# Sums of squares by head in the second layer of a four-layer transformer kernel: the head columns as stationary operand

## The reference, cut to what matters

```python
# B, L = 8, 256; H = 16 heads of 32; xin is the modulated layer norm of x
qkv = (xin @ Wqkv.T + qkv_bias).reshape(Bs, Lx, 3, H, D)
...
sm = jnp.exp(jnp.minimum(scale_mul_log, jnp.log(jnp.float32(100.0))))
qn = q / jnp.maximum(jnp.linalg.norm(q, axis=-1, keepdims=True), 1e-12) * sm
kn = k / jnp.maximum(jnp.linalg.norm(k, axis=-1, keepdims=True), 1e-12)
scores = jnp.einsum('bhqd,bhkd->bhqk', qn, kn) + attn_bias
p = jax.nn.softmax(scores, axis=-1)
```

## Time and profile before

| | |
|---|---|
| median of 3 runs | 2158.23 us (2153.22 to 2158.89) |
| the profiled execution | 2151.35 us, of which 2149.6 us are the span of the trace |
| PE busy | 1930.4 us, 90% |
| DVE, ACT, POOL busy | 1132.2, 1029.0, 785.8 us (53%, 48%, 37%) |
| mean granted clock of TensorE | 0.953 |
| the 32 chains of layer 1 | from 658 to 1589 us of the span |

### The profile page before, as it was taken

The page is one execution under the profiler, slowest core; times in us unless marked ns, Lnnn a source line. Parts: engine busy times, 40 slices in busy tenths (PEclk is TensorE's granted clock), DMA queues, the critical chain, the costliest instruction groups (busy, mean ns, idle before and its releaser), DMA issues.

```text
span 2149.6 us, 34826 instructions
## 1 busy us (share of the span) xinstructions
PE 1930.4 (90%) x12744; PEld 1512.8 (70%) x12744; DVE 1132.2 (53%) x3157; ACT 1029.0 (48%) x2450; POOL 785.8 (37%) x1093
## 2 busy tenths in 40 slices
PE   4778999999999999999899999979999989977875
PEld 2556777777888878788678777768875768745453
DVE  4656432653553365435674675574554675456442
ACT  3533332343333344443465465555567456477753
POOL 4454553211112443233577453336331432233220
PEclk9889999999999999999899999999999989989988
DMA  7234666545445533345345433424433424322310
GB/s 264 64 128 147 216 206 225 191 157 188 163 173 180 184 133 127 133 157 196 133 167 174 156 123 133 149 91 151 141 118 128 163 80 171 120 77 79 98 60 30
DMA packets 95097, 310.35 MB, mean 144 GB/s; under 512 B 10576, under 2 KB 11344, under 8 KB 93392
## 3 DMA queue, kind: packets, MB, share of 16 engines
q1 hardware_dynamic: 94928, 308.12, 41.4%
HBM read 241.50 MB, written 66.58 MB: 143 GB/s over the span
## 4 chain that ended last, share of the span: by engine, by line
PE 65%; DVE 13%; issue 7%; ACT 6%; POOL 6%; DMA 2%; SPq 0%; POOLq 0%; DVEq 0%; ACTq 0%
PE B L183 59%; PE B L186 6%; DVE SS L207 2%; DVE FB L204 2%; DMA ST<-in_wpack 2%; ACT SS L189 2%; POOL SS L198 1%; ACT FB L189 1%; POOL W L201 1%; POOL R L201 1%; DVE T L201 1%; DVE PT L195 1%; DVE FB L201 1%; ACT L189 1%; POOL W L198 1%
## 5 line engine op out<-in xcount | busy, mean ns | idle before, releaser
L198 POOL TENSOR_SCALAR SS<-SS,NM 128x256 f32<-128x256 f32 (+1 forms) x640 | 290.0, 470 | 829.4 <-DVE NM L213 829.3
L183 PE MATMUL B<-HM,W 128*128 128x512 f32 x2304 | 538.6, 394 | 15.6 <-DVE HM L204 8.7
L183 PEld LDWEIGHTS B<-HM,W 128*128 128x128 f32 x2304 | 438.8, 191 | 110.3 <-DVE HM L204 9.5
L183 PE MATMUL B<-G,W 128*128 128x512 f32 x1536 | 404.0, 414 | 29.7 <-DVE FB L204 9.8
L183 PEld LDWEIGHTS B<-G,W 128*128 128x128 f32 x1536 | 292.9, 196 | 103.9 <-issue 20.8
L189 ACT ACTIVATE SS<-SS,NM 128x256 f32<-128x256 f32 (+1 forms) x512 | 240.6, 471 | 218.1 <-DVE NM L198 217.8
L183 PE MATMUL B<-HA,W 128*128 128x512 f32 x864 | 222.3, 408 | 7.9 <-DVE HA L201 5.9
L186 PE MATMUL B<-ident,SS 128*128 128x128 f32 x1152 | 179.2, 294 | 40.3 <-POOL SS L198 27.8
L183 PEld LDWEIGHTS B<-HA,W 128*128 128x128 f32 x864 | 165.6, 196 | 46.9 <-DVE HA L201 6.3
L186 PEld LDWEIGHTS B<-ident,SS 128*128 128x128 f32 x1152 | 129.8, 147 | 76.1 <-POOL SS L198 34.2
L201 DVE TENSOR_TENSOR G<-FB,G 128x512 fp32r<-128x512 f32 x128 | 101.3, 793 | 155.2 <-ACT G L189 155.1
(11 more groups left out here) (108 smaller groups left out, 2658.7 us busy)
## 6 DMA issues: line engine op xcount, KB each, us to landing
W<-kept SPq DMA_DIRECT2D x357, 512.0 KB, 4.3
kept<-W SPq DMA_DIRECT2D x119, 512.0 KB, 4.6
ST<-in_wpack SPq DMA_DIRECT2D x135, 256.0 KB, 3.0
Y<-in_adaw SPq DMA_DIRECT2D x12, 1024.0 KB, 6.4
out_xT<-X SPq DMA_DIRECT2D x16, 256.0 KB, 2.1
X<-in_xT SPq DMA_DIRECT2D x1, 3072.0 KB, 14.6
FB<-in_pos SPq DMA_DIRECT2D x4, 256.0 KB, 7.6
X<-in_xT SPq DMA_DIRECT2D x1, 1024.0 KB, 6.7
```

Of the source, the lines that this page charges most:

```text
L183: return self.real.matmul(*a, **k) if self.real is not None else self
L198: return self.real.tensor_scalar(*a, **k) if self.real is not None else self
```

## The change

The sum of squares of a head is made with the operands exchanged. The head columns, padded by zeros to 32, are the stationary operand; each of the four 128x128 blocks of squares is the moving one, and the four results go to the four groups of 32 partitions of one bank, one column tile each. The sums then have the heads on the partitions, so two things are added: VectorE copies the 128x128 result into the scratch tile g, and PE transposes it once. The maximum that writes R16 reads 4 of each 32 columns of the transposed bank. The work is now in two steps, `sums` and `un2`. The head columns get a tile of their own (a view of CT, which is free by then) and a transfer of 16 KB in the step "bias". The positions of the q, k and v steps of layer 1 in `PLACE` are new.

```diff
-    "q1": [-1.273, 0.351, 1.427],
-    "k1": [0.902, 1.089, 2.211, 2.301, 3.616],
-    "v1": [3.958, 4.1],
+    "q1": [-1.372, -0.577, 0.6, 1.483],
+    "k1": [1.287, 0.51, 0.837, 2.25, 2.391, 3.618],
+    "v1": [3.809, 4.1],
...
             self.banked("un1", k, f, g)
             yield
+            self.banked("sums", k, g)
+            yield
             self.banked("un2", k, g)
...
+        heads = CT[:, 0, 0, :]
...
+                elif kind == "sums":
+                    k, g, u = a
+                    bank, sq = dp.buf(u), fr.buf(g)
+                    e.wait_ge(*s_heads.of())
+                    e.wait_ge(*a_qsq.of(*k))
+                    e.wait_ge(*dp.over(u))
+                    for j in range(4):
+                        r = e.matmul(bank[32 * j:32 * j + 32, 0:128], heads, sq[:, 128 * j:128 * j + 128],
+                                     start=True, stop=True)
+                    r.then_inc(*p_ss.up(*k))
                 elif kind == "un2":
                     k, g, u = a
-                    bank, sq = dp.buf(u), fr.buf(g)
-                    e.wait_ge(*a_qsq.of(*k))
+                    e.wait_ge(*d_ss.of(*k))
                     e.wait_ge(*dp.over(u))
-                    for m in range(4):
-                        r = e.matmul(bank[:, 4 * m:4 * m + 4], sq[:, 128 * m:128 * m + 128],
-                                     CV[:, COLS["head"]:COLS["head"] + 4], start=True, stop=True)
-                    r.then_inc(*p_ss.up(*k))
+                    e.transpose(dp.buf(u)[:, 0:128], fr.buf(g)[:, 0:128], ident[:, :]).then_inc(*p_sst.up(*k))
...
+                elif kind == "sums":
+                    k, g, u = a
+                    e.wait_ge(*p_ss.of(*k))
+                    e.tensor_copy(fr.buf(g)[:, 0:128], dp.buf(u)[:, 0:128]).then_inc(*d_ss.up(*k))
+                    dp.done(u, d_ss, *k)
...
-                    e.tensor_scalar(R16[:, x, 0, :], dp.buf(u)[:, 0:16], 1e-24, None, ALU.max).then_inc(*d_qmax.up(*k))
+                    e.tensor_scalar(R16[:, x, 0, :].rearrange("p (j h) -> p j h", j=4),
+                                    dp.buf(u)[:, 0:128].rearrange("p (j h) -> p j h", j=4)[:, :, 0:4], 1e-24, None,
+                                    ALU.max).then_inc(*d_qmax.up(*k))
...
+                    e.dma_start(heads, headsd).then_inc(*s_heads.up())
```

More of the change, by code:

```diff
@@ L70, in _cols @@
                     ("bfc1", 16), ("bfc2", 4), ("bada2", 8), ("emb_b", 8), ("ln_g", 4), ("ln_b", 4), ("out_b", 4),
-                    ("b1", 16), ("b2", 4), ("sml", 4), ("invf", 1), ("head", 4), ("quarter", 1)):
+                    ("b1", 16), ("b2", 4), ("sml", 4), ("invf", 1), ("quarter", 1)):
         COLS[name] = at
@@ L657, in spread, with program @@
         return out
-def program(nc, xT, pos, condT, biasd, cols, consts, tab2, wpack, adaw, out):
+def program(nc, xT, pos, condT, biasd, cols, consts, headsd, tab2, wpack, adaw, out):
     ctx = ExitStack()
@@ L721, in program @@
         s_st = [tally(f"s_st{k}", 16) for k in range(STAGES)]
-        s_ad, s_cv, s_ct, s_id, s_rot = (tally(x, 16) for x in ("s_ad", "s_cv", "s_ct", "s_id", "s_rot"))
+        s_ad, s_cv, s_ct, s_id, s_heads, s_rot = (tally(x, 16) for x in ("s_ad", "s_cv", "s_ct", "s_id", "s_heads", "s_rot"))
         p_adt, d_ad = tally("p_adt"), tally("d_ad")
@@ L726, in program @@
         p_ada, p_tot, p_var, p_bc = (tally(x) for x in ("p_ada", "p_tot", "p_var", "p_bc"))
-        p_qkv, p_rot, p_ss, p_nb = (tally(x) for x in ("p_qkv", "p_rot", "p_ss", "p_nb"))
+        p_qkv, p_rot, p_ss, p_sst, p_nb = (tally(x) for x in ("p_qkv", "p_rot", "p_ss", "p_sst", "p_nb"))
         p_sc, p_tr, p_va, p_out = (tally(x) for x in ("p_sc", "p_tr", "p_va", "p_out"))
@@ L742, in program @@
         d_trig, d_sin, d_qk, d_qhi, d_khi = (tally(x) for x in ("d_trig", "d_sin", "d_qk", "d_qhi", "d_khi"))
-        d_klo, d_qmax, d_ck = tally("d_klo"), tally("d_qmax"), tally("d_ck")
+        d_klo, d_ss, d_qmax, d_ck = tally("d_klo"), tally("d_ss"), tally("d_qmax"), tally("d_ck")
         d_max, d_neg, d_rec, d_pt, d_cx = (tally(x) for x in ("d_max", "d_neg", "d_rec", "d_pt", "d_cx"))
@@ L751, in program @@
         tallies = [
-            s_const, s_x0, s_x, s_pos, s_tab, s_out, *s_st, s_ad, s_cv, s_ct, s_id, s_rot, p_adt, d_ad, *s_w, p_ada, p_tot, p_var, p_bc, p_qkv, p_rot, p_ss,
+            s_const, s_x0, s_x, s_pos, s_tab, s_out, *s_st, s_ad, s_cv, s_ct, s_id, s_heads, s_rot, p_adt, d_ad, *s_w, p_ada, p_tot, p_var, p_bc, p_qkv, p_rot, p_ss, p_sst,
             p_nb, p_sc, p_tr, p_va, p_out, p_up, p_down, p_first, p_second, p_last, a_silu, a_sm, a_sq,
@@ L755, in program @@
             a_y, d_ada, d_sm, d_gb, d_sum, d_sub, d_sq, d_var, d_nmul, d_nlo, d_trig,
-            d_sin, d_qk, d_qhi, d_khi, d_klo, d_qmax, d_ck, d_max, d_neg, d_rec, d_pt, d_cx, d_xo, d_gate, d_glo,
+            d_sin, d_qk, d_qhi, d_khi, d_klo, d_ss, d_qmax, d_ck, d_max, d_neg, d_rec, d_pt, d_cx, d_xo, d_gate, d_glo,
             d_xd, d_tg, d_xl, g_const, g_whi, g_wlo, g_rstd, g_cos, g_qlo, g_qr, g_norm, g_xb]
@@ L1250, in vector @@
                     x = 0 if k[0] == "q" else 1
-                    e.wait_ge(*p_ss.of(*k))
+                    e.wait_ge(*p_sst.of(*k))
                     if k[2:] != (0, 0):
                         e.wait_ge(*a_wide.of(k[0], 1, *divmod(4 * k[2] + k[3] - 1, 4)))
-                    e.tensor_scalar(R16[:, x, 0, :], dp.buf(u)[:, 0:16], 1e-24, None, ALU.max).then_inc(*d_qmax.up(*k))
+                    e.tensor_scalar(R16[:, x, 0, :].rearrange("p (j h) -> p j h", j=4),
+                                    dp.buf(u)[:, 0:128].rearrange("p (j h) -> p j h", j=4)[:, :, 0:4], 1e-24, None,
+                                    ALU.max).then_inc(*d_qmax.up(*k))
                     dp.done(u, d_qmax, *k)
@@ L1812 @@
         _vec(g["L3_cond_b1"].reshape(-1)), _vec(g["L3_cond_b2"].reshape(-1)), _vec(rep),
-        np.tile(inv, 4)[:, None], np.repeat(np.eye(4, dtype=f), 32, axis=0),
+        np.tile(inv, 4)[:, None],
         np.full((128, 1), math.pi / 2)], axis=1)
@@ L1838 @@
         "cols": np.ascontiguousarray(cols.astype(f)),
-        "consts": consts, "tab2": tab2, "wpack": wpack, "adaw": adaw,
+        "consts": consts, "headsd": np.repeat(np.eye(4, 32, dtype=f), 32, axis=0), "tab2": tab2, "wpack": wpack, "adaw": adaw,
     }
```

## The result

| | before | after |
|---|---|---|
| median | 2153.59 us (6 runs, 2147.18 to 2158.89) | 2167.38 us (6 runs, 2165.94 to 2168.82) |
| profiled execution | 2151.35 us | 2167.59 us |
| mean granted clock | 0.953 | 0.947 |

The ratio is 1.0067, with a 95% interval of 1.0054 to 1.0079: slower by 0.67%, some 14 us. The forecast was 2160 us and "no change". The time lies in the range that holds 8 in 10 (2147 to 2171) and 2.4 us above the forecast's own range (2152 to 2165). The call was wrong: the difference is a little over twice what can be told from nothing.

What follows compares the result with a forecast made beforehand. PE, busy 90% of the span, was taken as the bound; 10.9 us spared against 13.8 us of waits, at 77%, gave +2.2 us, on a 2158.2 us median 2160 us, "no change"; own range 2152 to 2165, 8 in 10 2147 to 2171.

Steps and rivals of the forecast that it cites:

- the sum: Balance of PE time spared (10.9 us) against added waits (13.8 us), each passed on at 77%: +2.2 us.
- The sums on TensorE: PE's block of 8 passes in four column tiles takes 0.35 us, not 0.81; 0.17 us of it fixed.
- The transpose: PE's added transpose in each of 32 chains: 0.12 us, 0.20 as upper end where it stands alone between products.
- The waits: PE waits 5.5 us before `un3` at four queries and 4.3 us before `sums` at keys right behind their product.
- the lag: DVE starts R<-B or the key's copy late, adding 0 to 1.9 us wherever little lies between; taken as 4 us.
- the four short queries: Places 1 and 2, piece 2 tile 3, piece 1 tile 3: PE waits 1.75, 1.85, 1.15, 0.8 us before `un3`.
- rival 2: Slower: DVE's lag at its upper end, about 11 us, waits passed on in full; +10 us, 2168 us; chance 0.20.
- The pass-on at 77%: Only 77% of spared time and waits reaches the end, PE's share of the first stretch's last-ending chain.
- Rival 1: Faster: the waits don't stand where put, at most a third come; 2143 to 2151 us, middle 2149; chance 0.29.
- rival 3: Slower or no gain: column tiles of a block of 8 don't overlap; +11, about 2170 us; chance 0.06.

Runs made afterwards that it cites:

- e2: The changed kernel at the positions of before, with the exchanged operands alone, no copy and no transpose (numbers wrong): ratio 0.9960 to the kernel before.
- e11: The changed kernel with the query's `un2` and `un3` back at their positions of before: 2173.9 us, ratio 1.0099 to the kernel before.
- e12: e11 with ACT issuing the query's spread behind the key's two activations instead of before them: 2156 us, ratio 1.0012 to the kernel before.
- e3: The whole change at the positions of before, with the `sums` steps added: 2177.4 us, ratio 1.0115 to the kernel before.
- e1: The kernel before, with the old sums, at the new query, key and value positions: 2174.7 us, ratio 1.0100 to the kernel before.
- e5: The kernel before with the query's new positions alone: ratio 1.0058 to the kernel before.
- e6: The kernel before with the key's new positions alone: ratio 1.0013 to the kernel before.
- e8: The change for the queries only, at the positions of before, keys keeping the old sums: 2147.5 us, ratio 0.9979 to the kernel before.

## Why the prediction was right and wrong

**The measured size lies in the range, the call "no change" was wrong**, and the failed step is the sum: its waits were too small, and a cost of the clock was not in it. It was 10.9 us spared against 13.8 us of waits, both passed on at 77%: -8.4 + 10.6 = +2.2 us. In the stage it is 5.6 us less work and 16.8 us more idle time, +11.2.

That the time lies in the range is in part luck. 2160 us stands on the median of three runs, 2158.2. The median of six is 2153.6; from there the forecast is 2156 and its wide range ends at 2166, below the measured 2167.4. The change forecast was +2 us, the measured one is +13.8.

*The sums on TensorE: right.* 0.35 us a block were taken; it is 0.36 before a product and 0.24 before B<-PT,V. The four column tiles overlap. The drain of the Trainium skill's page "TensorEngine Tiling (Array Packing)", "Key Properties", never costs more here than the 0.17 us a block that the rows before had shown: the whole block takes 0.24 to 0.36 us. At nine of the 32 places B<-PT,V follows, which has the same tiling.

*The transpose: within its bounds on the whole.* 0.12 us were taken, 0.20 as the upper end. A lone one takes 0.02 to 0.03 us from start to start between products and 0.27 before a wait, and at the full clock the kernels with transposes have 0.3 to 2.4 us more work than e2 for all 32 of them. The sign that was named, PE's busy time falling by 10 us or more, did not come: it fell by 5.6 us in the stage and rose from 1930.4 to 1931.5 over the span. Outside the stage it is 6.7 us more, and there lie 17 of the 28 us more at the lower clock.

*The waits: right in kind, short in size, and one link was missing.* Foretold were 5.5 us before `un3` and 4.3 us before the sums; measured are 9.6 us more before B<-ident,FB, 7.3 before B<-FB,CT, and 4.2 before B<-few,T in the stage, which had no price: 21.1 against 13.8 with the lag. At the four short queries PE waits 0.91, 2.81, 2.26 and 1.42 us, 7.4 in all, but three of the four are released by DVE's CX and only one (2.26, at place 2) by the spread. I counted PE's work between `un2` and `un3` against the chain through DVE, POOL and ACT, and saw PE as the only one who waits. But ACT waits there as well, for up to 5.4 us, and behind it stand the key's activations and the context of an earlier unit, with a bank that PE needs. The prediction named this sort of question for DVE and left it out for ACT. e11 tests the count by itself and refutes it; e12 shows what stands in its place.

*The lag: put on the wrong engine.* 4 us were taken, and rival 2 had DVE's lag at 11 us or more. Only 1.1 us of idle time are released by the copy. The measured time lies where rival 2 was, but its mark, over 4 us released by DVE FB L195, is missing: the rival is not what happened. It does happen at the old positions (e3, 23.5 us).

*The pass-on at 77%: near for the waits, wrong for the work.* Of the 21.1 us of new idle time in three groups 16.8 are left in the stage, 80%, since other groups have 4.3 us less. That this is near 77% is not shown to be more than chance. Of 8.9 us of work spared at the full clock 5.6 are left: the other 3.3 are the estimate for work at the lower clock, a cost that was not in the sum at all. One block of 12 matmuls at 1090.90, behind the wait of 2.81 us, took 2.1 us more.

*Rival 1* (the waits don't stand there) and *rival 3* (the sum isn't cheaper) are refuted by the rows.

What stays open: how 21.5 us of e1 divide among query, key and value positions beyond the 12 and 3 of e5 and e6; how much of the loss is the bank of `values`, which no run changes by itself; and whether the 5.0 us outside the stage are more than the spread between executions.

## What to carry to other kernels

When a step is moved closer to its consumer, list for each in-order engine that takes part what stands behind the waiting instruction, and who needs its bank or tile; the longest operation of the chain (here 2.9 us on POOL) holds all of them, and the order on the holding engine may be worth more than the distance (e12: one instruction, 18 us). An operation that is exchanged for a cheaper one with a turned result pays for the turning: little in the work of turning it back (0.3 to 2.4 us for 32 transposes here), much in a round trip for which the place must be there; here queries had it and keys had not (e8 against e3). And two stretches can only be compared where they begin and end at the same instruction, and a block's cost is read from start to start: 0.27 us of busy time were 0.03 us or less here.

## What the runs showed of the hardware

A block of 8 short fp32 passes in four column tiles costs TensorE no more per pass than one of 32: 0.24 us before another block of the same tiling, 0.03 us a pass, as in 32 passes in 1.01 us. Before a product it is 0.36 us. One transpose between two products takes 0.02 to 0.03 us from start to start, though it is busy for 0.27.

Behind a pause of 2.81 us the granted clock was 0.54 over the next 7 us, and behind one of 3.37 us (e5) it was 0.50 for 9 us, and the blocks took twice their time. At place 1, behind 1.93 us, the key's B<-PT,V right after it still took 0.99 us, the full speed; the clock fell later, behind two more pauses of 0.91 and 0.55 us, and was 0.51 from 795 to 802 us. Before the change it fell at place 1 too, for a shorter time, where PE had paused for only 0.55 us at 788.84. The changed kernel and then the kernel before:

```profile
792.60:795.00 2.40, 1.84 (x24) 1.79 (x28) 2.37 (x12) 0.33 (x1) 0.34 (x2) 1.00 0.10 38
795.00:802.00 7.00, 5.93 (x39) 4.69 (x32) 4.79 (x18) 4.72 (x17) 6.75 (x7) 0.51 0.00 0
```

```profile
788.90:792.30 3.40, 3.40 (x32) 2.81 (x32) 1.44 (x5) 2.37 (x9) 3.24 (x2) 0.50 0.03 10
```
